# Output projection of a mixture-of-experts layer: expert weights loaded in groups behind the attention heads, output bias added to the source rows two stages earlier

## The reference

```python
x  = x + layernorm(agent_attention(layernorm(x)))
src = layernorm(x)
q, k, v = src @ Wq + bq, src @ Wk + bk, src @ Wv + bv        # 16 heads of 16 channels
heads = softmax(q @ k.T * 16 ** -0.5) @ v
y  = src + (heads @ Wo + bo)
xf = layernorm(y, ln1_g, ln1_b)
gates = softmax(xf @ gW + gb)                                # 8 experts, the best 2 of each row
ff = sum over the 2 chosen experts e: gate_e * (relu(xf @ W1[e] + b1[e]) @ W2[e] + b2[e])
x  = x + layernorm(layernorm(xf + ff, ln2_g, ln2_b))
```

## Time and profile before

| | us |
|---|---|
| median of 3 runs | 3812.51 |
| lowest and highest | 3805.7 and 3818.8 |
| profiled execution, its own time | 3818.61 |
| span of the profiled execution | 3816.9 |
| TensorE busy in the span | 3298.5 (86%) |
| VectorE busy | 2927.6 (77%) |
| ScalarE busy | 2057.6 (54%) |
| GpSimd busy | 1173.3 (31%) |

### The profile page before, as it was taken

How to read it: one execution, slowest core, us unless ns; L and a number is a source line. 1 busy time by engine, 2 the same in 40 slices (tenths; PEclk the granted TensorE clock), 3 DMA queues, 4 the chain that set the end, 5 groups by cost and what they waited for, 6 DMA issues and landing times. The chain is left out here.

```text
span 3816.9 us, 87664 instructions
## 1 busy us (share of the span) xinstructions
PE 3298.5 (86%) x34938; PEld 1884.3 (49%) x34939; DVE 2927.6 (77%) x4552; ACT 2057.6 (54%) x2972; POOL 1173.3 (31%) x910
## 2 busy tenths in 40 slices
PE   4769999999999999968699775997799999747876
PEld 1433333333333333326466552343687787546665
DVE  5659999998999999706344254676699999868986
ACT  0316777776777777833011155665565766334553
POOL 0100000000000000005100270000799999747775
PEclk8868999998999999967899866998899999879998
DMA  1674023030303120043222253333543434211110
GB/s 55 220 187 47 13 42 46 8 48 6 48 4 49 20 34 5 5 154 118 79 65 64 75 160 117 112 124 133 138 132 116 133 116 134 90 57 50 55 33 17
DMA packets 221875, 296.93 MB, mean 78 GB/s; under 512 B 56377, under 2 KB 154946, under 8 KB 219842
## 3 DMA queue, kind: packets, MB, share of 16 engines
q1 hardware_dynamic: 204258, 258.24, 25.1%
q0 software_dynamic: 6144, 17.05, 1.4%
q10 hardware_dynamic: 11120, 16.62, 1.3%
HBM read 174.75 MB, written 116.47 MB: 76 GB/s over the span
## 5 line engine op out<-in xcount | busy, mean ns | idle before, releaser
L921 DVE TENSOR_REDUCE att_maxima<-att_ps_m 128x1 f32<-128x512 f32 x2048 | 1286.4, 684 | 90.8 <-PE att_ps_m L977 89.3
L876 ACT ACTIVATE att_probs<-att_ps_s 128x1024 f32<-128x1024 f32 x1024 | 1000.0, 1022 | 289.9 <-PE att_ps_o L1004 276.7
L1004 PE MATMUL att_ps_o<-att_probs,att_vs 128*32 128x256 f32 x8192 | 662.6, 396 | 4.8 <-ACT att_probs L876 0.6
L977 PE MATMUL att_ps_m<-att_ks,att_qs 48*128 48x512 f32 x2048 | 587.3, 515 | 29.3 <-DMA att_ks<-scratch_k 28.6
L2235 POOL TENSOR_TENSOR ss_ch<-ss_h,ss_c_rep 128x1024 f32<-128x1024 f32 x256 | 601.6, 2416 | 12.4 <-DVE ss_h L2322 12.4
L2354 PE MATMUL ss_ps_u<-ss_diag,ss_dx_t 128*32 128x128 f32 x16384 | 476.0, 275 | 28.1 <-DMA ss_dx_t<-scratch_dx_t 14.6
L2354 PEld LDWEIGHTS ss_ps_u<-ss_diag,ss_dx_t 128*32 128x32 f32 x16384 | 454.2, 111 | 84.8 <-issue 63.9
L977 PEld LDWEIGHTS att_ps_m<-att_ks,att_qs 48*128 48x128 f32 x2048 | 238.7, 189 | 477.0 <-DVE att_maxima L921 393.6
L992 PE MATMUL att_ps_s<-att_qs,att_ks 50*128 50x512 f32 x2048 | 456.7, 407 | 4.0 <-DMA att_qs<-att_m_parts 1.2
L2274 ACT ACTIVATE ss_decay<-ss_delta,ss_a_neg 128x1024 f32<-128x1024 f32 x256 | 293.9, 1148 | 232.1 <-DVE ss_h L2322 210.1
L1004 PEld LDWEIGHTS att_ps_o<-att_probs,att_vs 128*32 128x32 f32 x8192 | 163.0, 108 | 365.1 <-issue 342.3
(11 more groups left out here) (391 smaller groups left out, 4472.6 us busy)
## 6 DMA issues: line engine op xcount, KB each, us to landing
ss_delta<-scratch_delta SPq DMA_DIRECT2D x256, 128.0 KB, 3.1
att_qs<-scratch_q SPq DMA_DIRECT2D x96, 128.0 KB, 9.3
att_ks<-scratch_k SPq DMA_DIRECT2D x96, 128.0 KB, 10.7
ex_x<-scratch_sorted_x SPq DMA_DIRECT2D x72, 132.0 KB, 2.1
scratch_sorted_y<-ex_y SPq DMA_DIRECT2D x72, 128.0 KB, 1.7
scratch_v<-qkv_v_ext SPq DMA_DIRECT2D x8, 1024.0 KB, 4.4
scratch_q<-qkv_parts SPq DMA_DIRECT2D x16, 512.0 KB, 5.3
scratch_k<-qkv_parts SPq DMA_DIRECT2D x16, 512.0 KB, 6.0
```

What stands on the lines that cost most here:

```text
L876: act.activation(probs[:, (2 * n + pair) % 4, :, :], ps_s[pair][:, :, :], ACT.Exp, scale=HD ** -0.5).then_inc(exp_done, 1)
L921: dve.tensor_reduce(maxima[:, j, at:at + 1], ps_m[plan.bank(key)][:, :], AX.X, ALU.max).then_inc(maxed, 1)
L977: pe.matmul(ps_m[plan.bank(key)][:, :], qs[own, s // QC % 2, s % QC, p, t * P:(t + 1) * P], ks[own, s // QC % 2, p, c * GN:(c + 1) * GN], ...
L1004: mm = pe.matmul(ps_o[h * VW:(h + 1) * VW, cols], vs[st // QC % 2][:, kt, h * VW:(h + 1) * VW], probs[:, (2 * n + h // 2) % 4, h % 2, cols ...
```

## The change

In project_qkv, bo is loaded too, over all partitions. GpSimd gets a second function, add_out_bias, which adds bo to the normalised rows of a group and writes them into a new buffer src_b; SP stores src_b in place of src. VectorE, before it overwrites a slot of src, waits for the GpSimd add of two groups earlier, where it waited for the store.

In attention_output, the bias matmul and its operands go. SP's order is new: heads 0, Wo (with a semaphore of its own), source rows 0, heads 1, the four small loads, and then for each group the next source rows, the heads of two groups ahead, and W1 and W2 of one expert; b1 comes last. ScalarE issues no transfers. The waits for the small loads move to where they are first used in group 0, and the final wait for the weights moves from ScalarE to SP.

```diff
@@ project_qkv @@
+        src_b = r.sb("src_b", [P, 2, GT, C])
...
+                sp.dma_start(bo[:, 0, :], over(io["bo"], [P, C])).then_inc(loaded, 16)
...
-                        sp.wait_ge(src_ready, (g + 1) * GT)
-                        sp.dma_start(rows_at(scratch.src, at), src[:, slot, :, :]).then_inc(src_stored[slot], 16)
+                        sp.wait_ge(src_biased, g + 1)
+                        sp.dma_start(rows_at(scratch.src, at), src_b[:, slot, :, :]).then_inc(src_stored[slot], 16)
...
-                pool.wait_ge(loaded, 6 * 16)
+                pool.wait_ge(loaded, 7 * 16)
+
+                def add_out_bias(g, slot):
+                    pool.wait_ge(src_ready, (g + 1) * GT)
+                    pool.wait_ge(src_stored[slot], (g // 2 + 1) * 16)
+                    pool.tensor_tensor(src_b[:, slot, :, :], src[:, slot, :, :], over(bo[:, :, :], [P, GT, C]), ALU.add).then_inc(src_biased, 1)
...
-                run_stages(pool, GROUPS, (add_bias, 1))
+                run_stages(pool, GROUPS, (add_out_bias, 0), (add_bias, 1))
...
-                    dve.wait_ge(src_stored[slot], (g // 2 + 1) * 16)
+                    if third_on(g):
+                        dve.wait_ge(src_biased, g - 1)
@@ attention_output @@
-                for dst, name in ((wo, "Wo"), (gw, "gW")):
-                    sp.dma_start(dst[:, :, :], io[name].rearrange("(k p) c -> p k c", p=P)).then_inc(loaded, 16)
-                sp.dma_start(bo[:, :], io["bo"]).then_inc(loaded, 16)
...
+                def load_experts(e):
+                    sp.dma_start(route.w1[:, e, :, :], io["W1"][e:e + 1, :, :].rearrange("o (k p) f -> p (o k) f", p=P)).then_inc(w_loaded, 16)
+                    sp.dma_start(route.w2[:, e, :, :], io["W2"][e:e + 1, :, :].rearrange("o (k p) c -> p (o k) c", p=P)).then_inc(w_loaded, 16)
+
+                load_heads(0, 0)
+                sp.dma_start(wo[:, :, :], io["Wo"].rearrange("(k p) c -> p k c", p=P)).then_inc(wo_loaded, 16)
+                load_src(0, 0)
+                load_heads(1, 1)
+                sp.dma_start(gw[:, :, :], io["gW"].rearrange("(k p) c -> p k c", p=P)).then_inc(loaded, 16)
...
-                run_stages(sp, GROUPS, (load_heads, -2), (load_src, -1), unroll=True)
+                for g in range(GROUPS):
+                    if g + 1 < GROUPS:
+                        load_src(g + 1, (g + 1) % 2)
+                    if g + 2 < GROUPS:
+                        load_heads(g + 2, g % 2)
+                    load_experts(g)
+                sp.dma_start(route.b1[:, :], over(scratch.b1_rows, [P, E * FF])).then_inc(late_loaded, 16)
...
+                sp.wait_ge(w_loaded, 2 * E * 16)
+                sp.wait_ge(late_loaded, 16)
...
-                for e in range(E):
-                    act.dma_start(route.w1[:, e, :, :], io["W1"][e:e + 1, :, :].rearrange("o (k p) f -> p (o k) f", p=P)).then_inc(w_loaded, 16)
-                    act.dma_start(route.w2[:, e, :, :], io["W2"][e:e + 1, :, :].rearrange("o (k p) c -> p (o k) c", p=P)).then_inc(w_loaded, 16)
-
-                act.dma_start(route.b1[:, :], over(scratch.b1_rows, [P, E * FF])).then_inc(late_loaded, 16)
...
                 def product(g, slot):
+                    if g == 0:
+                        pe.wait_ge(wo_loaded, 16)
...
-                            pe.matmul(ps_y[:, t, :], heads_t[:, k, t * P:(t + 1) * P], wo[:, k, :], start=k == 0, stop=False)
-                        mm = pe.matmul(ps_y[:, t, :], one[:, :], bo[:, :], start=False, stop=True)
+                            mm = pe.matmul(ps_y[:, t, :], heads_t[:, k, t * P:(t + 1) * P], wo[:, k, :], start=k == 0, stop=k == KC - 1)
```

More of the change, by code:

```diff
@@ L535, in project_qkv @@
         v_ready, v_copied, v_biased = r.sem("v_ready"), r.sem("v_copied"), r.sem("v_biased")
+        src_biased = r.sem("src_biased")
         x1_stored, src_stored, parts_stored, v_stored = ([r.sem(f"{n}{slot}") for slot in range(2)]
@@ L639, in _ @@
             def _(pe):
-                pe.wait_ge(loaded, 6 * 16)
+                pe.wait_ge(loaded, 7 * 16)
                 def products(g, slot):
@@ L1089, in attention_output @@
         wo, gw = r.sb("wo", [P, KC, C]), r.sb("gw", [P, KC, E])
-        bo, gb, one = r.sb("bo", [1, C]), r.sb("gb", [P, 1, E]), r.sb("one", [1, P])
+        gb = r.sb("gb", [P, 1, E])
         before = r.sb("before", [P, E, E])
@@ L1143, in load_src @@
                     sp.dma_start(src[:, slot, :, :], rows_at(scratch.src, g * GN)).then_inc(src_loaded[slot], 16)
-                run_stages(sp, GROUPS, (load_heads, -2), (load_src, -1), unroll=True)
+                def load_experts(e):
[6 more added lines that the diff above has]
+                sp.dma_start(gw[:, :, :], io["gW"].rearrange("(k p) c -> p k c", p=P)).then_inc(loaded, 16)
+                sp.dma_start(gb[:, 0, :], over(io["gb"], [P, E])).then_inc(loaded, 16)
+                with nc.allow_non_contiguous_dma("gain and shift by channel"):
+                    for dst, name in ((route.gain, "ln1_g"), (route.shift, "ln1_b")):
+                        sp.dma_start(dst[:, :], io[name].rearrange("o (k p) -> p (o k)", p=P)).then_inc(loaded, 16)
+                for g in range(GROUPS):
[5 more added lines that the diff above has]
+                sp.dma_start(route.b1[:, :], over(scratch.b1_rows, [P, E * FF])).then_inc(late_loaded, 16)
                 sp.wait_ge(ends_copied, 1)
@@ L1164, in _ @@
                                    pattern=[[1, P]], channel_multiplier=-1).then_inc(route_set, 1)
-                pool.memset(one[:, :], 1.0).then_inc(route_set, 1)
                 pool.memset(zeros[:, :], 0.0).then_inc(route_set, 1)
@@ L1193, in _ @@
                 NORM_STEPS = STATS_STEPS + SCALE_STEPS
-                dve.wait_ge(loaded, 6 * 16)
                 dve.wait_ge(before_set, 2)
-                dve.wait_ge(route_set, 11 + 2 * E)
+                dve.wait_ge(route_set, 10 + 2 * E)
                 def shift_logits(g, slot):
                     c = Chain(dve, gate_steps, g * GATE_STEPS)
+                    if g == 0:
+                        dve.wait_ge(loaded, 4 * 16)
                     dve.wait_ge(g_ready, g + 1)
```

20 lines of the change are left out of this document (10 added, 10 removed).

## The result

The changed kernel takes 3760.9 us (median of 4 runs, 3746.8 to 3773.8), the kernel before, timed beside it, 3815.7 (4 runs): a ratio of 0.987 [0.985, 0.990] (the two medians alone give 0.986). A second set gave 3757.0 and 0.987 [0.985, 0.989]. The forecast was 3766 (3753 to 3792).

A forecast was written before the change was run, and what follows sets the result against it. Bound: a series of stages; in the projection, late heads and ScalarE's issues, then TensorE, then GpSimd's scatters. -22.6 - 13.2 - 3 - 8.0 = -46.8 us from 3818.6 gives 3772, or 3766 from the median 3812.5; range 3753 to 3792.

The forecast's parts named there:

- Start of the projection: Output projection's start: heads first in SP's queue and no ScalarE issues bring the first product forward, -22.6 us.
- Bias matmuls and clock: Projection before the first scatter: removed one-row bias matmuls give -13.2 us, an earlier rise of TensorE's clock -3 us.
- I take -3 us: Clock term in the projection's products: a value between a rise 5.7 us into product 0 (-7.3) and no gain (0).
- best bounds of the two terms together: Projection before the first scatter: most favourable values, -14.2 us for bias matmuls and -7.3 for the clock.
- my other bound: Clock term, unfavourable case: the clock falls in the two following groups that ran high before, +6 us.
- The series of scatters: Projection's last part: from the first scatter on, smaller gaps shorten 91.3 us to 83.3, -8.0 us (bounds -9.2 and 0).
- the first interval falls to VectorE's own 9.4 and the three to 32.3: Scatter series: slot intervals of groups 0 to 4 shrink to 41.7 us against GpSimd's pace of 40.5.
- Weights in groups: Projection: expert weights issued by SP group by group behind the heads cost nothing on the path, 0 us.
- q, k, v stage, 0: q, k, v stage: eight GpSimd bias adds are covered, by 0.1 us at worst, costing 0 us.
- that rival: q, k, v stage: GpSimd's adds block VectorE on the path, full price +18.9 us, giving 3785; chance 0.07.
- The sum: Whole change: all terms together, -46.8 us, all of it expected from the projection stage.

The follow-up runs named there:

- bias_only: Kernel before with only the output bias moved to the source rows, all loads in the old order; 3783.0 us, ratio 0.994.
- order_only: Kernel before with only the new order of loads, the bias still a one-row matmul in the projection; 3776.1 us, ratio 0.991.
- after: The changed kernel itself, in its first profiled execution, against the kernel before; median 3760.9 us, ratio 0.987.
- scatter_last: Changed kernel with every scatter held back until the slots of all 8 groups are there; 3795.1 us, ratio 0.996.
- before_third: The kernel before, unchanged, profiled a third time; its projection stage took 192.2 us.
- weights_last: Changed kernel with all expert weights and b1 issued only after the rows of zeros; 3787.8 us.
- plain_stores: Kernel with all scatters held back, plus 64 plain stores by SP in the scatters' old place; 3792.5 us, ratio 0.997.
- half_product: Changed kernel with half of each output-projection product left out; 3754.6 us.
- before_again: The kernel before, unchanged, profiled a second time; its projection stage took 201.2 us.
- after_again: The changed kernel, unchanged, profiled a second time; its projection stage took 146.9 us.
- warm: Changed kernel with 14 more identity transposes on TensorE ahead of the projection's first wait; 3762.8 us, ratio 0.987.
- scatter_one_late: Changed kernel with the first scatters held back until the slots of group 1 are there too; 3769.1 us, ratio 0.991.

## Why the prediction was right, and where it was not

*Start of the projection, -22.6.* Right: -23.0 (30.1 to 7.05 us from the stage's start). Transposes 3.95 us after it (4.4 forecast), product 3.1 behind them, as the sum had it.

*Bias matmuls and clock, -13.2 and -3.* The mechanism was right and the clock's share mis-sized. From first product to first scatter it was 54.5 us before and 33.2 after: -21.4 instead of -16.2. bias_only alone gives -21.2 (1672.31 to 1705.64), and in order_only, with the one-row matmuls, the same stretch took 56.5. No run splits the 21.4 us between the matmuls and the clock. The failing step, as far as the trace tells, is "I take -3 us": the clock rose 4 us into product 0 and read 1.00 for 41 us, beyond the first scatter, near the best bounds of the two terms together (-21.5). The rise in the q, k, v stage was the right model and should have been taken at full value; the fall in groups 2 and 3 that my other bound allowed for did not come. The first scatter came 44.4 us earlier, not 38.8.

*The series of scatters, -8.0.* Wrong in sign on the forecast's own execution (90.3 to 97.6), and about zero against what the kernel before usually does (98.0 in the mean of three, 95.8 for the two of after). The failed step is "the first interval falls to VectorE's own 9.4 and the three to 32.3 [...] GpSimd is then the bound of this part". VectorE's own pace is right: 9.0 us a group in scatter_last, and the series without gaps is 80.0. In the changed kernel the first interval was 9.1, but the next three took 44.7 us. What the sum lacked is the disturbance beside the indirect scatters. Reading the 10.4 us of gaps of before as TensorE's load was not the error: that execution has no late signal, and before_third shows such gaps without one. The error was to assume that nothing else would take their place. Executions of the kernel before have 10, 18 or 27 us of gaps, and my single profile had the least disturbed of the three.

*Weights in groups, 0; q, k, v stage, 0.* Both right. The weights: weights_last. The q, k, v stage: 129.3 against 129.2, but for another reason than mine. I had VectorE's subtractions blocked and saved by 0.1 us; they aren't blocked at all, and a second add costs 3.1 us in 8 groups. The full price of that rival, +18.9, was carried over from an instruction on 128x4 to unlike ones. The Trainium skill (SBUF — State Buffer, SBUF: two separate sides) gives the exclusive lock a condition that my rival left out: outside VectorE's two-port modes it concerns instructions with two SBUF inputs, against a GpSimd instruction that reads SBUF. The trace agrees: the 128x4 instruction, with both sources in SBUF, was held for 2.31 us, and the subtractions, whose first source is the buffer that TensorE writes (qkv_ps_qk, in PSUM), took 0.70 us each beside the add.

*The sum.* The projection took 146.6 and 146.9 us against 183.7, 201.2 and 192.2: 45.6 us less in the means, with -46.8 forecast. That is nearer than the terms deserve, by luck: 5.6 us more at the first scatter and about 6 less in the series (in the means) cancel, and the execution of before was itself the fastest of three in this stage. The medians differ by 54.8. The rest, some 9 us, lies in stages that the change doesn't touch. Head attention ranged from 1406 to 1424 us over 14 executions, the stage behind the experts from 173 to 189; with three executions of before, two of them the slowest in head attention, I can't tell whether any of it belongs to the change. This stays open.

*What stays open of the disturbance.* Shown: it needs the indirect scatters in flight (scatter_last), not their bytes (plain_stores), not the weights (weights_last), not TensorE's full load (half_product); its late signals start 7 to 12 us after the first scatter in every kernel without one-row matmuls that has scatters beside the groups. With one-row matmuls it came late or not at all (order_only's and before_third's first late signal 61 and 63 us behind the first scatter), but in before_again after 12 us. What in an indirect transfer does it, and what the granted clock, which often falls in the same microsecond, has to do with it, was not separated. Slow loading of instructions isn't seen: from 1700 to 1710 us the instruction queues moved one piece (0.02 MB, 0.9% of the time of 16 engines), and from 1690 to 1710 us of scatter_last, without disturbance, one of that size at 0.4% of twice the time. When a piece was asked for isn't recorded, so this rival isn't excluded.

## What to carry to other kernels

Look at what stands ahead of the first useful load in each queue, and on each engine that also computes: here it cost 23 us, and the weights behind the heads cost nothing. A stage whose waits vary between executions can't be costed from one profile: take two or three of the kernel before, and treat the waits in the least disturbed one as a floor. And when an engine gets faster beside another's indirect transfers, ask first whether it was ever undisturbed there.

## What the hardware did that I had not expected

- One-row matmuls between full ones kept TensorE at 0.50 for 34 us of nearly full work (order_only: busy 31.5 of 32.6 us); in nine executions without them it read 1.00 from 3 to 5 us into the first product on, in the tenth (warm) from before it.
- Beside GpSimd's indirect scatters TensorE issued single matmuls 0.7, 1.4 or 2.1 us apart, and its signals came up to 10 us late (12 in scatter_one_late), even at a DMA share of 0.29 (weights_last). With 64 plain stores of like size, issued by SP, there was nothing of it, and groups 0 to 4 followed each other by 9.0 us instead of 12.5 and 13.5 (after_again and after).
- GpSimd's add of 128x1024 does not slow VectorE's 128x512 subtractions that read a PSUM buffer (0.70 us each with and without it), while it held a 128x4 one for 2.31 us.
